# A graph network on one core: eleven dense chunks in place of ten in layer 0, and two late table portions

## What is computed

```
h = relu(h @ enc_w1.T + enc_b1) @ enc_w2.T + enc_b2
def step(h, w):                      # five times
    m = h @ w
    agg = segment_sum(m[src], dst)
    gi = agg @ gru_wih.T + gru_bih
    gh = h @ gru_whh.T + gru_bhh
    r, z = sigmoid(ir + hr), sigmoid(iz + hz)
    n = tanh(i_n + r * h_n)
    return (1 - z) * n + z * h
h = relu(h)
out = x + sigmoid(relu(h @ dec_w1.T + dec_b1) @ dec_w2.T + dec_b2)
```

## Time and profile before

| | |
|---|---|
| three runs | 5216.20, 5216.44, 5221.04 us |
| median | 5216.44 us |
| profiled execution | span 5215.6 us from first to last instruction |
| layer 0, from the profile | about 158 to 1402 us |
| layers 1 to 4 | 950, 952, 952 and 960 us |
| TensorE busy (modelled) | 90% of the span |
| GpSimd, ScalarE, VectorE busy | 72%, 69%, 44% |

### The profile page before, as it was taken

How to read it: one execution, slowest core, us unless ns; L and a number is a source line. 1 busy time by engine, 2 the same in 40 slices (tenths; PEclk the granted TensorE clock), 3 DMA queues, 4 the chain that set the end, 5 groups by cost and what they waited for, 6 DMA issues and landing times.

```text
span 5215.6 us, 63622 instructions
## 1 busy us (share of the span) xinstructions
PE 4702.7 (90%) x21332; PEld 3526.3 (68%) x21332; DVE 2294.8 (44%) x5897; ACT 3622.8 (69%) x3301; POOL 3776.4 (72%) x3931
## 2 busy tenths in 40 slices
PE   5589999999899999988999999899999979999997
PEld 2356666666577777767777777677777767777775
DVE  7677877777333333332333333333333333333333
ACT  3477878777577777757767676667777657777773
POOL 2577777777577777767777777677777767777776
PEclk8799999999899999999999999999999989999998
DMA  6898888989877777787777778777777876777674
GB/s 203 263 271 258 257 256 264 266 254 282 257 213 232 221 222 226 222 280 226 224 222 227 220 219 291 223 213 228 220 229 220 261 248 205 221 213 219 212 223 139
DMA packets 700236, 1218.94 MB, mean 234 GB/s; under 512 B 272657, under 2 KB 429330, under 8 KB 699810
## 3 DMA queue, kind: packets, MB, share of 16 engines
q1 hardware_dynamic: 511888, 700.98, 44.0%
q0 software_dynamic: 187616, 512.28, 31.9%
q10 hardware_dynamic: 434, 1.81, 0.1%
HBM read 1025.79 MB, written 188.94 MB: 233 GB/s over the span
## 4 chain that ended last, share of the span: by engine, by line
POOL 47%; PE 24%; issue 17%; DMA 5%; ACT 4%; DVE 3%; POOLq 0%; DVEq 0%; SPq 0%; ACTq 0%
POOL messages L885 47%; PE four_ps L1819 11%; PE four_ps L1803 3%; PE agg_ps L1725 3%; ACT counts L1057 2%; DMA messages<-table,src_stage 2%; ACT room L1037 1%; DMA h_old<-states 1%; DMA adjacency<-room 1%; PE agg_ps L1732 1%; PE r_ps L1764 0%; DVE gate_r L1247 0%; PE z_ps L1764 0%; PE r_ps L1769 0%; PE z_ps L1769 0%
## 5 line engine op out<-in xcount | busy, mean ns | idle before, releaser
L885 POOL DMA_INDIRECT messages<-table,src_stage x3887 | 3742.6, 963 | 1353.8 <-issue 1169.0
L1057 ACT ACTIVATE counts<-raw 128x2048 fp32r<-128x2048 uint8 x1736 | 2840.9, 1691 | 592.4 <-PE four_ps L1819 428.6
L1819 PE MATMUL four_ps<-counts,parts 128*128 128x512 f32 x12152 | 3043.1, 405 | 83.9 <-ACT counts L1057 47.8
L1819 PEld LDWEIGHTS four_ps<-counts,parts 128*128 128x128 f32 x12152 | 2294.2, 191 | 660.1 <-issue 162.4
L1346 DVE TENSOR_TENSOR selection<-agg_ps,dst_stage 128x1024 fp32r<-128x1024 bf16 (+1 forms) x489 | 594.6, 1216 | 2220.3 <-PE agg_ps L1732 2219.4
L1725 PE MATMUL agg_ps<-messages,selection 128*128 128x256 f32 x3887 | 629.3, 307 | 250.3 <-DMA messages<-table,src_stage 249.6
L1725 PEld LDWEIGHTS agg_ps<-messages,selection 128*128 128x128 f32 x3887 | 534.6, 198 | 290.5 <-DMA messages<-table,src_stage 289.6
L1037 ACT ACTIVATE room<-four_ps 128x392 uint16<-128x392 f32 x832 | 363.5, 496 | 145.9 <-PE four_ps L1803 120.1
L1370 DVE TENSOR_REDUCE rows<-agg_ps 128x128 f32<-128x256 f32 x489 | 203.0, 415 | 292.7 <-PE agg_ps L1725 292.6
L997 ACT ACTIVATE gate_r<-r_ps,b_rz 128x512 f32<-128x512 f32 (+1 forms) x125 | 84.8, 678 | 305.7 <-PE r_ps L1747 264.0
L1732 PE MATMUL agg_ps<-place,rows 128*128 128x192 f32 x978 | 242.3, 329 | 15.4 <-DVE rows L1370 15.4
(11 more groups left out here) (203 smaller groups left out, 3129.8 us busy)
## 6 DMA issues: line engine op xcount, KB each, us to landing
raw<-adjacency SPq DMA_DIRECT2D x868, 448.0 KB
adjacency<-room SPq DMA_DIRECT2D x104, 784.0 KB, 6.2
parts<-table SPq DMA_DIRECT2D x35, 1792.0 KB, 13.2
messages<-table,src_stage POOLq DMA_INDIRECT x3887
table<-table_stage SPq DMA_DIRECT2D x108, 512.0 KB, 5.6
h_old<-states SPq DMA_DIRECT2D x120, 256.0 KB
states<-h_new SPq DMA_DIRECT2D x108, 256.0 KB, 3.2
table<-room SPq DMA_DIRECT2D x12, 512.0 KB, 3.0
```

What stands on the lines that cost most here:

```text
L885: nc.gpsimd.indirect_dma_start(messages[:, slot, t, :, :].rearrange("p i f -> p (i f)").bitcast(F32), None, table[k.layer % 2], bass.Indir ...
L1057: nc.scalar.activation(to, raw[:, p % 2, :, a * EIGHTH:e * EIGHTH].rearrange("p q (k d) -> p k q d", d=EIGHTH), ACT.Copy).then_inc(expande ...
L1819: last = mm(strip_ps, parts[:, block, half, :], counts[:, 0 if k.first else p % 2, at, :], start=(p == 0 and at == 0 and half == 0), stop= ...
```

## The change

`FIRST_DENSE` goes from 10 to 11. Layer 0 then has 11 strips, 14 more pieces (28 units, 196 matmuls of L1819) and 8 gathered groups (64 gathers) less: 108 steps in place of 116, with strips and sets ending at step 100 in place of 108. Chunk 10 was gathered and is now the last strip. Its rows lie in portion 2 (blocks 28 to 41) and portion 3 (blocks 42 to 55), since it spans blocks 40 to 43; so `late_portion` becomes `late_portions`, a list. In the layers after, the list has one entry, as before.

```
-FIRST_DENSE = 10
+FIRST_DENSE = 11
...
-    def late_portion(self):
-
-        return (self.dense * J - 1) // PORTION
+    def late_portions(self):
+
+        return list(range((self.dense - 1) * J // PORTION, (self.dense * J - 1) // PORTION + 1))
...
-            late = (Stage(self.layer - 1).late_portion(), PORTIONS - 1)
-            order = [portion for portion in range(PORTIONS) if portion not in late] + list(late)
+            late = Stage(self.layer - 1).late_portions() + [PORTIONS - 1]
+            order = [portion for portion in range(PORTIONS) if portion not in late] + late
...
-                late = k.late_portion()
+                late = k.late_portions()
                 for portion in range(PORTIONS - 1):
                     used = (k.dense - 1) * PIECES + 2 * portion + 2
-                    if portion != late and k.pieces_to(step - 2) < used <= k.pieces_to(step - 1):
+                    if portion not in late and k.pieces_to(step - 2) < used <= k.pieces_to(step - 1):
                         next_portion(k, portion)
                 if step == k.gru_at[k.dense - 1] + 5:
-                    next_portion(k, late)
+                    for portion in late:
+                        next_portion(k, portion)
```

## The result

The changed kernel takes **5269.01 us**, the median of 4 runs (5267.53 to 5270.08). The kernel before takes 5217.57 us on the same chip, the median of 4 runs (5216.2 to 5221.04). The ratio is 1.0095, with a 95% interval of 1.0081 to 1.011: the change makes the kernel slower by 51 us. The forecast was 5265 us, slower.

A forecast was written before the change was run, and what follows sets the result against it. The prediction took PE's stream to bound layer 0, with POOL's gathers hidden behind it. Its terms, 49.3 + 4.8 - 10.2 + 7.0 - 2 = +48.9 us, took 5216.4 to 5265 us, range 5240 to 5288 us.

The forecast's parts named there:

- What bounds layer 0: In layer 0 PE's stream sets the pace and POOL's gathers are hidden, so taking away 64 gathers (82 us) gains nothing.
- The two counts of the backlog, 10 and 27: Layer 0: tiles gathered by POOL but not yet summed by PE, 10 up to 600 us, 27 up to 1300 us.
- Rival 1: In layer 0 the gather stream is the bound and PE follows it: 75 us faster, 5141 us; chance 5%.
- The strip, +49.3 us: On PE in layer 0, one added strip costs 14 pieces at 3.52 us each: +49.3 us.
- The waits around a strip, +4.8 us: PE's waits in layer 0 at strip ends and for sets' copies grow by one strip's share: +4.8 us.
- the -2 us for portion 3 in the run-up: In layer 0's run-up, portion 3 no longer takes its turn, which gives back PE waits: -2 us.
- 8 groups, -10.2 us: On PE in layer 0, 8 gathered groups fewer at 1.28 us each save 10.2 us.
- The sets, nothing: In layer 0 the same 416 sets move into fewer steps, with the same work: no change in time.
- The end, +7.0 us: At layer 0's end the last chunk's old state queues behind 3.6 MB instead of 1.8: +7.0 us.
- Rival 2 (ACT): In layer 0 ACT becomes what PE waits for: +94 us, 5310 us at full price; chance of more than +72 us 12%.
- Rival 3 (waits take the strip in): PE's 62 us of waits in layer 0 absorb 39 us of added work: 5223 us; chance 5%.
- What was said to show it: Signs in the changed profile: layer 0 ends at 1451 us, POOL waits over 100 us for sums, old state about 12 us.

## Why the prediction was right

The forecast of 5265 us with 5240 to 5288 met 5269.01. Point by point:

- **What bounds layer 0.** Read from the counts of gathers and sums, this held on the chip of the trace. POOL's wait for sums went from 3.0 to 154.3 us, and the run with half the gathers and ten strips shows directly that 464 gathers taken away bring 24 us, 15.5 of them before step 10. The two counts of the backlog, 10 and 27, were a lucky pair: at 650 us it was already 17. Rival 1 (gathers are the bound, 5141 us) fell here. The Trainium skill's sentence that it was weighed with ("Trainium Kernel Development and Optimization", section "Best Practices") is about the distance to the roofline. It doesn't say which engine sets the pace, and this trace shows the difference: weight loads were busy for only 745 of 1244 us in the layer that PE's stream bounded.
- **The strip, +49.3 us.** The price held: 3.52 us a piece stands in the changed trace too, and 196 matmuls at the 251 ns of the upper clock level are 49.2 us. What the forecast left out is the clock. It had no term for it, and the units took 56.9 us more, of which 6.8 come from 38 more matmuls at the lower level. PE waited longer at most strip ends, as in the place shown above, where the new order leaves it less other work, and the clock fell after seven of those waits. The 131 ns a matmul of the Trainium skill ("TensorE: Matmul & The Clock Gate", section "Back-to-back issue gap") does not hold for this form: 14 take 3.19 us in the chain after, 228 ns each.
- **The waits around a strip, +4.8 us.** The strip ends cost more than expected, +9.8 us: not one more wait of 2.1 us, but longer ones at most of the old strip ends as well. But from 290 us on the waits for set copies fell by 15.0 us and those for counts by 4.9, and PE's idle time as a whole changed by -1.6 us. A likely reason, argued and not shown, is that the same number of sets now stands among more units, so that ACT has more time for each copy. I had scaled both kinds with the number of strips; only the strip ends go with it. This, with the -2 us for portion 3 in the run-up that was set apart, is 4.4 us too much.
- **8 groups, -10.2 us.** Measured -8.6 us, from start to start. The other groups took a little longer.
- **The sets, nothing.** Measured -3.0 us.
- **The end, +7.0 us.** Measured +6.1 from the last sum to the first gather, and +6.3 on the old state itself (5.49 to 11.79). Both the mechanism (128 KB behind 1.8 MB more in one queue) and the rate held. Issuing the state first shows that the queue is the cause: the wait goes, and comes back on the next store.
- **The sum.** Strip, waits, groups and relief were +41.9 us and came out as +46.1; the end was +7.0 and came out as +6.1. That the sum is only 3 us low is in part luck: units 7.6 us, groups 1.6 and other work on PE 2.4 came out higher than forecast, waits 4.4 and sets 3.0 lower. The mechanism and the price of a strip were right; the clock was missing.
- **Rival 2 (ACT).** Waits for widened counts went down to 9.2 us, against the tens of us that it needed. **Rival 3 (waits take the strip in)** needed idle time that shrinks by 39 us; it shrank by 1.6.
- **What was said to show it.** Old state 12 us, other layers unchanged: right. Layer 0 ended at 1456.5 us instead of 1451. By the first gather of layer 1 it is 52.1 us more instead of 49; the rest is that the 1451 was reckoned from a rounded 1402, where that gather stood at 1404.4. POOL's waits came to 154 us instead of 126: I had counted 82 + 44 us. Of the 28 us more, 4 are the longer stretch, and 12 were counted elsewhere before: the idle pieces between gathers fell by 31.5 us (279.7 to 248.2), where 64 fewer of them explain 19.5. Some 10 more are the gathers themselves, busy for 73.6 us less (917.10 to 843.53), where 64 at the old mean are 63.0. The backlog was to reach 32 tiles before the middle of the layer: it did, at 500 us.

What the prediction did not say, and the runs show, is that it holds for chips like the one of the trace. On a chip that ran the kernel before in 6320 us, the change is a gain.

## What to carry to other kernels

Where two engines are both busy nearly all the time, count what the one has made and the other has used at two or three times: a backlog that grows by more than one group names the slower one, even if it has never been waited for. Price added work on TensorE by the times from one start to the next, not by busy time, in which overlap counts twice: the same two units are 3.52 us by the one and 3.84 by the other. Then ask what the new order leaves PE to do at its waits, and look at the granted clock after each of them. And a small load behind large ones in one queue costs the large ones' whole transfer time; putting it ahead helps only if nothing wanted stands behind them.

## What the runs showed of the hardware that was not expected

**The clock fell at short waits.** In the changed kernel the granted clock went from the upper (2.4 GHz) to the lower level (1.2 GHz) at waits of 1.6 to 4.8 us of an otherwise busy PE, twelve times between step 10 and the last sum, for 51 us in all; before, five times and 20 us. This cost the units 6.8 us more than before, a seventh of the price of the strip. Not every such wait was followed by it: a wait of 2.96 us at 483 us was not.

**Chips differ more than the change.** The same kernel before took 5217.57 and 5222.96 us on two chips and 6261.15, 6320.02 and 6329.57 on three others, and the sign of the change turned with it. The differences from the kernel before are, on the slow chips, nine strips +111 us, eleven -38 us, 116 fewer gathers -108 to -112 us; on the fast ones, eleven strips +51 us and 464 fewer gathers -24 us. In layer 1 on a slow chip (kernel with two late portions):

```profile
1757.00:2900.00 1143.00, 946.88 (x3872) 710.79 (x3872) 309.27 (x675) 663.95 (x478) 705.69 (x740) 0.89 0.62 192
```

ACT, DVE and POOL are busy for as long as in the fast row (663.93, 309.24 and 704.86 us in the second row of this document's first fence) over 1143 us in place of 950. The instructions are not slower; what stands between them is longer. PE's matmuls take longer (946.88 against 872.88 us) at a granted clock of 0.89 against 0.97. Not all of what stands between is one engine waiting for another. PE also pauses in the middle of a unit, where its matmuls wait for nobody:

```profile
2002.47 3.63 PE L1822 MATMUL four_ps<-counts,parts 128*128 128x512 f32 x13
2007.83 0.40 PE L1822 MATMUL four_ps<-counts,parts 128*128 128x512 f32 x1 [1.73 <-issue]
```

This trace has 176 pauses inside units, of up to 2.1 us and 133 us together, and 124 inside group sums, 98 us together. Every trace from a slow chip has as many or nearly so (128 to 191 inside units, 91 to 133 us), and none of the four traces from the two fast chips has one. What makes PE pause is not shown and stays open. So does why the gathers count on those chips, though POOL has 275.1 us of waits for sums in the change's run.

**Half the gathers make the first ten steps of the layer faster.** From 158 to 300 us PE did 325 matmuls before, and 396 with half the gathers:

```profile
158.00:300.00 142.00, 79.10 (x325) 46.06 (x326) 91.19 (x309) 51.29 (x105) 106.57 (x106) 0.71 0.90 277
```

```profile
158.00:300.00 142.00, 88.13 (x396) 54.39 (x396) 99.73 (x337) 63.89 (x123) 62.69 (x65) 0.81 0.85 256
```

The DMA share is 0.90 and 0.85, and the granted clock is 0.71 and 0.81: PE is less often idle, and more of the stretch runs at the upper of its two levels. Whether the DMA engines or the wait for the first rows hold the early steps was not separated.
